# One unrolled stream of 96 attention units, with the feed-forward in pieces between later units, for a cross-attention and six-layer transformer kernel

## What is computed

```python
x = x + xattn(layernorm(x), ctx)              # 16 batch elements, 128 tokens, 128 features
x = x + ffn_stack(layernorm(x))
# ffn_stack:
for i in range(6):
    x = attn_layer(shift_tokens(x), Wqkv[i], q_scale[i], k_scale[i], Wo[i]) + x
    x = ffn_layer(shift_tokens(x), ln_g[i], ln_b[i], W1[i], b1[i], W2[i], b2[i]) + x
# shift_tokens: the upper 64 features of a token are those of the token before it
# attn_layer: 16 heads of 64; q and k l2-normalised, scaled, rotary; each token sees itself and
#   the 32 before it; softmax; times v; times Wo (1024 x 128)
# ffn_layer: layernorm, W1 (128 x 682), a * gelu(gate), W2 (341 x 128)
```

## Time and profile before

| | |
|---|---|
| three runs | median 2150.25 us (2150.19 to 2153.46) |
| profiled execution, first to last instruction (span) | 2147.6 us |
| PE busy | 2027.4 us, 94% |
| DVE busy | 1735.7 us, 81% |
| ACT busy | 1552.4 us, 72% |
| POOL busy | 1353.9 us, 63% |
| DMA | 21.08 MB, mean 10 GB/s |
| mean granted clock of PE | 0.977 of 2.4 GHz |

### The profile page before, as it was taken

How to read it: one execution, slowest core, us unless ns; L and a number is a source line. 1 busy time by engine, 2 the same in 40 slices (tenths; PEclk the granted TensorE clock), 3 DMA queues, 4 the chain that set the end, 5 groups by cost and what they waited for, 6 DMA issues and landing times.

```text
span 2147.6 us, 44268 instructions
## 1 busy us (share of the span) xinstructions
PE 2027.4 (94%) x14352; PEld 1593.7 (74%) x14352; DVE 1735.7 (81%) x3845; ACT 1552.4 (72%) x4966; POOL 1353.9 (63%) x1884
## 2 busy tenths in 40 slices
PE   7699999899999889999999999988999999999997
PEld 5477777777777767777777777776777777777776
DVE  4688887788888678888778888867888867888876
ACT  3488887378888558888738888846888864888873
POOL 2477666466766547777547666745766664766661
PEclk8799999999999999999999999999999999999999
DMA  3000000000000010000010000001000000000000
GB/s 98 30 9 0 0 0 1 17 36 1 0 0 0 11 35 9 0 0 0 1 44 9 0 0 0 0 11 35 9 0 0 0 4 11 1 0 0 0 0 20
DMA packets 11920, 21.08 MB, mean 10 GB/s; under 512 B 1659, under 2 KB 9518, under 8 KB 11054
## 3 DMA queue, kind: packets, MB, share of 16 engines
q1 hardware_dynamic: 11822, 19.77, 2.9%
HBM read 18.72 MB, written 1.05 MB: 9 GB/s over the span
## 4 chain that ended last, share of the span: by engine, by line
PE 68%; DVE 14%; ACT 7%; issue 6%; POOL 4%; DVEq 0%; DMA 0%; ACTq 0%; SPq 0%; POOLq 0%
PE ps L371 15%; PE ps L378 7%; PE ps L351 7%; PE ps L389 7%; PE ps L359 6%; ACT pr L633 6%; PE ps L397 5%; PE ps L353 5%; PE ps L352 5%; PE ps L367 3%; PE ps L520 3%; DVE nmax L966 3%; DVE xs L924 1%; PE ps L341 1%; DVE hT L1052 1%
## 5 line engine op out<-in xcount | busy, mean ns | idle before, releaser
L633 ACT ACTIVATE pr<-ps,nbias,rn 128x128 f32<-128x128 f32 x1536 | 682.4, 454 | 204.6 <-DVE nbias L970 199.4
L784 POOL TENSOR_TENSOR pr<-pr,rsum 128x512 f32<-128x512 f32 x384 | 395.4, 1039 | 304.0 <-DVE rsum L974 304.0
L759 POOL TENSOR_TENSOR t<-t 128x512 f32<-128x512 f32 x384 | 485.1, 1273 | 65.3 <-DVE t L950 59.1
L371 PE MATMUL ps<-kT,qT 64*128 64x128 f32 x3072 | 445.1, 285 | 0.0
L371 PEld LDWEIGHTS ps<-kT,qT 64*128 64x128 f32 x3072 | 371.6, 188 | 97.5 <-issue 97.5
L966 DVE TENSOR_REDUCE nmax<-ps 128x4 f32<-128x512 f32 x384 | 258.7, 674 | 67.2 <-PE ps L371 67.1
L633 ACT ACTIVATION_READ_ACCUMULATOR pr<-ps,nbias,rn 128x1 f32 x1536 | 306.3, 199 | 0.0
L351 PE MATMUL ps<-w_hi,xt_hi 128*128 128x512 f32 x576 | 280.5, 487 | 23.1 <-DVE t L950 18.1
L948 DVE TENSOR_TENSOR t<-ps,rope 128x512 f32<-128x512 f32 x384 | 261.2, 680 | 8.7 <-ACT sq L609 8.7
L950 DVE TENSOR_TENSOR t<-ps,rope 128x512 f32<-128x512 f32 x384 | 260.5, 678 | 0.0
L934 DVE TENSOR_REDUCE ss<-sq 128x8 f32<-128x512 f32 x384 | 248.8, 667 | 3.5 <-issue 2.6
(11 more groups left out here) (116 smaller groups left out, 3173.9 us busy)
## 6 DMA issues: line engine op xcount, KB each, us to landing
wqkv<-wqkv_in SPq DMA_DIRECT2D x6, 1536.0 KB, 8.4
wo<-wo_in SPq DMA_DIRECT2D x6, 512.0 KB, 3.6
w<-w_in SPq DMA_DIRECT2D x6, 342.0 KB, 3.0
w<-w_in SPq DMA_DIRECT2D x6, 172.5 KB
x<-x_in SPq DMA_DIRECT2D x4, 256.0 KB, 4.2
out<-x SPq DMA_DIRECT2D x4, 256.0 KB, 2.3
ctx<-ctx_in SPq DMA_DIRECT2D x4, 240.0 KB, 3.8
qks<-qk_scale_in SPq DMA_DIRECT2D x6, 64.0 KB, 2.8
```

The source lines that it names most:

```text
L371: i = mm(ps[:, o, k * P:(k + 1) * P], qT[r, par, h // 2, :], kT[r, par, h // 2, :], start=False, stop=k == 3, skip_group_check=True)
L633: i = A(pr[:, g, k, :], ps[:, S_BANK[g], k * P:(k + 1) * P], ACT.Exp, bias=nbias[:, g, k:k + 1], scale=rn[:, par, g // 2, 0, 2 * k + g % 2 ...
L759: G.tensor_tensor(t1[:, c, :], t1[:, c, :], t2[:, c, :], ALU.add).then_inc(qk_added[c], 1)
L784: G.tensor_tensor(w, w, rsum[:, g, :].unsqueeze(2).broadcast_to([P, 4, P]), ALU.mult).then_inc(pr_ready[g], 1)
```

## The change

- **One stream.** The layer loops and their special first and last steps go. Steps s = -4 to 107 are unrolled. Step s holds pieces of units s to s-3, of any layer: unit u has layer u // 16. `bank_free` and the waits take unit numbers.
- **Feed-forward between units.** A quad f (0 to 23) has its pieces at fixed distances: its shift and its transposition in step 4f+6, statistics to the first gate in 4f+7, gates 1 and 2 in 4f+8, `ffn_down` in 4f+10, the residual in 4f+11; the next layer's input is transposed for a whole quad in 4f+12. Since the engines' steps are not aligned, DVE's `ffn_stats` (step 4f+7) stands ahead of PE's `ffn_transpose` (step 4f+6).
- **Scores on two row halves.** `scores(u, h2)` makes the two mask products of a half (two banks), and then the eight heads in the order even, odd, even, odd. `row_max` and `inverse_sum` take both banks of a half at once (1024 columns).
- **Token shift by DMA.** SP copies the quad's residual into `xsh`: 64 features of 127 partitions, one partition down, and 64 features of 128 partitions. PE's two shift products and the shifted identity go. DVE's `copy_x` goes too: PE transposes `xr` directly, a quad at a time.
- **Tables.** `ffn_gate` loads Gelu's tables ahead of chunk 0 and the set with Exp and Ln after chunk 2; in between exponentials and norms of attention units are run.
- **Weights.** The next layer's split of Wqkv moves from POOL into the last unit of a layer: high parts on ACT, low parts on DVE (Q0, Q1, V0) and POOL.
- **Copies.** DVE takes six of the 512-column copies of a unit (before four), ACT six (before eight).
- **SP's order.** Weight loads and shift copies share SP's one queue in a fixed order.

```diff
-            def scores(l, b, par, g):
...
-                mm(ps[:, o, :], ident16[:], band16[:].rearrange("p a k -> p (a k)"), start=True, stop=False, skip_group_check=True)
-                for k in range(4):
-                    h = head(g, k)
-                    r = slice(E * (h % 2), E * (h % 2) + E)
...
+            def scores(u, h2):
+
+                pe.wait_ge(tq_ready[2 * h2], u + 1)
+                pe.wait_ge(tq_ready[2 * h2 + 1], u + 1)
+                for odd in range(2):
+                    mm(ps[:, S_BANK[odd], :], ident16[:], band16[:].rearrange("p a k -> p (a k)"), start=True, stop=False,
+                       skip_group_check=True)
+                for k in range(4):
+                    for odd in range(2):
+                        r = slice(E * odd, E * odd + E)
+                        i = mm(ps[:, S_BANK[odd], k * P:(k + 1) * P], qT[r, par(u), 4 * h2 + k, :], kT[r, par(u), 4 * h2 + k, :],
+                               start=False, stop=k == 3, skip_group_check=True)
+                        if k == 3:
+                            i.then_inc(s_ps[h2], 1)
...
+            def shift_tokens(f):
+
+                s = slice(f % NQ * QUAD, f % NQ * QUAD + QUAD)
+                sp.wait_ge(x_updated, f * QUAD + QUAD)
+                if f >= 1:
+                    sp.wait_ge(f_xh, f)
+                else:
+                    sp.wait_ge(const_ready, 9)
+                sp.dma_start(xsh[1:P, :, E:P], xr[0:P - 1, s, E:P]).then_inc(f_shifted, 16)
+                sp.dma_start(xsh[:, :, 0:E], xr[:, s, 0:E]).then_inc(f_shifted, 16)
...
-            with sp.Fori(1, L) as l:
-                wait_apart(sp, w_ready, l * 6)
-                sp.dma_start(wqkv[:], wqkv_d[l]).then_inc(ld_qkv, 16)
...
+            for l in range(L):
+                if l >= 1:
+                    load_rest(l)
+                if l + 1 < L:
+                    load_qkv(l + 1)
+                    load_scales(l + 1)
+                shift_tokens(NQ * l)
+                shift_tokens(NQ * l + 1)
+                if l + 1 < L:
+                    load_w1(l + 1)
+                shift_tokens(NQ * l + 2)
+                if l + 1 < L:
+                    load_wo(l + 1)
+                shift_tokens(NQ * l + 3)
...
+            def load_rest(l):
+                if l >= 1:
+                    sp.wait_ge(f_y_ps, l * NQ)
+                    sp.wait_ge(f_h, l * NQ * FCH)
+                sp.dma_start(w2[:], w2_d[l]).then_inc(ld_ffn, 16)
+                sp.dma_start(vec[:], vec_d[l]).then_inc(ld_ffn, 16)
...
-            def ffn_shift(l, q):
...
-                mm(o[:, :, 0:E], ident, xr[:, s, 0:E], start=True, stop=True)
-                mm(o[:, :, E:P], shift, xr[:, s, E:P], start=True, stop=True).then_inc(f_shift_ps, 1)
...
+            def ffn_gate(f, c):
+                if c == 0:
+                    nc.scalar.preload_act_table(ACT.Gelu)
+                j = f * FCH + c
+                act.wait_ge(f_h_ps, j + 1)
+                A(gate[:, j % 2, :], ps[0:FC, GATE_BANK, :], ACT.Gelu, bias=vec[0:FC, 2 + FCH + c:3 + FCH + c]).then_inc(f_gate, 1)
+                if c == FCH - 1:
+                    nc.scalar.preload_act_table_set("natural_log_exp_and_others")
...
+            def ffn_stats(f):
+                dve.wait_ge(f_shifted, 32 * (f + 1))
+                for b in range(QUAD):
+                    V.bn_stats(st[:, f % 2, b, :], xsh[:, b, :]).then_inc(f_stats, 1)
+                dve.wait_ge(f_stats, 4 * (f + 1))
+                aggregate(f).then_inc(f_var, 1)
...
+            def upper_w(u, c):
+
+                if u % B == B - 1 and u + 1 < UNITS:
+                    l = layer_of(u) + 1
+                    w = slice(CHUNK_COLS[c], CHUNK_COLS[c] + 512)
+                    act.wait_ge(ld_qkv, 16 * (l + 1))
+                    act.wait_ge(qkv_ps[c], u + 1)
+                    A(w_hi[:, w], wqkv[:, w], ACT.Copy).then_inc(w_hi_ready[c], 1)
```

The steps of DVE, as written in the change (the numbers are the distances s - u or s - 4f):

```diff
+            def step(s):
+                run_input(s, 15, lower_xt)
+                run_quad(s, 7, ffn_stats)
+                run(s, 2, row_max, 1)
+                run(s, 1, rotary, K1)
+                run(s, 3, copy_o, 0)
+                run_quad(s, 7, ffn_normalise)
+                run(s, 1, rotary, Q1)
+                run(s, 1, lower_w, Q1)
+                run_quad(s, 7, ffn_affine)
+                run(s, 1, sum_squares, Q1)
+                run(s, 1, sum_squares, K1)
+                run_quad(s, 8, ffn_gated, 1)
+                run(s, 1, copy_qk, K0)
+                run(s, 3, copy_o, 1)
+                run(s, 1, clamp_norm, 1)
+                run(s, 1, copy_v, 0)
+                run(s, 0, rotary, Q0)
+                run(s, 0, lower_w, Q0)
+                run(s, 1, row_max, 0)
+                run_quad(s, 7, ffn_lower)
+                run(s, 2, inverse_sum, 1)
+                run(s, 0, rotary, K0)
+                run(s, 2, copy_pT, 1)
+                run(s, 1, lower_w, V0)
+                run(s, 3, add_residual)
+                run(s, 0, sum_squares, K0)
+                run(s, 1, copy_qk, K1)
+                run(s, 0, sum_squares, Q0)
+                run_quad(s, 11, ffn_residual)
+                run(s, 0, clamp_norm, 0)
+                run(s, 1, inverse_sum, 0)
+                run_quad(s, 7, ffn_gated, 0)
+                run_quad(s, 8, ffn_gated, 2)
+                for l in range(1, L):
+                    if at(s, -8, l):
+                        rope_tables(l)
```

More of the change, by code:

```diff
@@ L199, in bank_free @@
-    def bank_free(eng, l, i, *users):
-        for semaphore, lag in users:
-            if live(i, lag):
-                eng.wait_ge(semaphore, nth(l, i - lag))
-                return
-    def x_ahead(i):
-        return isinstance(i, int) and i <= 1
-    def first_element(b):
-        return isinstance(b, int) and b == 0
-    def last_step(i):
-        return isinstance(i, int) and i == STEPS - 1
-    def steps(eng, l, step):
-        for i in range(1, HEAD_STEPS):
-            step(l, i, i % 2)
-        with eng.Fori(0, (STEPS - HEAD_STEPS - TAIL_STEPS) // 2) as j:
-            step(l, 2 * j + HEAD_STEPS, 0)
-            step(l, 2 * j + (HEAD_STEPS + 1), 1)
-        for i in range(STEPS - TAIL_STEPS, STEPS):
-            step(l, i, i % 2)
@@ L227, in all_layers @@
[L227 to L236 removed]
+    f_shifted, f_stats, f_var, f_sum, f_rstd, f_xh, f_xhT_ps, f_xhT, f_h_ps, f_gate, f_h, f_y_ps = (
+        sem("f_" + s) for s in ("shifted", "stats", "var", "sum", "rstd", "xh", "xhT_ps", "xhT", "h_ps", "gate", "h", "y_ps"))
+    c_stats, c_var, c_sum_eps, c_rstd, c_xn, c_tr_ps, c_tr, c_qk_ps, c_qk, c_s_ps, c_max, c_exp, c_sum, c_pn, c_pT_ps, c_pT, c_o_ps, c_x1 = (
+        sem("c_" + s) for s in ("stats", "var", "sum_eps", "rstd", "xn", "tr_ps", "tr", "qk_ps", "qk", "s_ps", "max", "exp", "sum", "pn",
+                                "pT_ps", "pT", "o_ps", "x1"))
@@ new lines, in build, with live, run, due @@
+    f_hi, f_lo, w1_hi_ready, w1_ready = sem("f_hi"), sem("f_lo"), sem("w1_hi_ready"), sem("w1_ready")
+    final_sum, stored = sem("final_sum"), sem("stored")
+    FIRST_STEP, LAST_STEP = -4, 108
+    def live(s, lag):
+        return 0 <= s - lag < UNITS
+    def run(s, lag, task, *args):
+        if live(s, lag):
+            task(s - lag, *args)
+    def due(s, lag, first=0, last=QUADS):
+        return (s - lag) % QUAD == 0 and first <= (s - lag) // QUAD < last
+    def run_quad(s, lag, task, *args):
+        if due(s, lag):
+            task((s - lag) // QUAD, *args)
@@ new lines, in step @@
+            def step(s):
+                run(s, 0, rotate, K0)
+                run(s, 0, lower_w, K0)
+                run(s, 2, normalise_p, 3)
+                run(s, 0, rotate, Q0)
+                run_quad(s, 6, ffn_power)
+                run(s, 1, normalise_p, 0)
+                run(s, 0, refine_norm, 0)
+                run(s, 1, normalise_p, 1)
+                run(s, 0, normalise_k, 0)
+                run(s, 0, rotate, K1)
+                run(s, 0, lower_w, K1)
+                run(s, 0, rotate, Q1)
+                run(s, 1, lower_w, V1)
+                run(s, 0, refine_norm, 1)
+                run(s, 0, normalise_k, 1)
+                run(s, 1, normalise_p, 2)
+                for l in range(L):
+                    if at(s, 5, l):
+                        split_w1(l)
@@ L838, in _ @@
-            pool.wait_ge(const_ready, 8)
-            step(0, 0, 0)
-            all_layers(pool, layer)
+                    split_first_weights(c)
+                    split_first_weights(c + 1)
+            pool.wait_ge(const_ready, 9)
+            for s in range(FIRST_STEP, LAST_STEP):
+                step(s)
         @block.vector
@@ L1121, in add_input @@
-            def add_input(q):
-                s = slice(q * QUAD, (q + 1) * QUAD)
-                dve.wait_ge(x_final, L * NQ + q + 1)
-                V.tensor_tensor(x1[:, s, :], x1[:, s, :], xr[:, s, :], ALU.add).then_inc(final_sum, 1)
-            rope_tables(0)
-            copy_x(0, 0, 0)
```

(8 more changed lines are left out.)

1033 lines of the change are left out of this document (453 added, 580 removed).

## The result

| | before | after |
|---|---|---|
| median of the runs | 2150.7 us (2150.19 to 2153.46, 4 runs) | 2326.1 us (2316.83 to 2327.28, 4 runs) |
| span of the profiled execution | 2147.6 us | 2322.5 us |
| mean granted clock of PE | 0.977 | 0.910 |

The change makes the kernel **slower by 8.1%**: ratio 1.081, 95% interval 1.079 to 1.084. The forecast was slower by 1.2%, 2176 us, within 1990 to 2290.

The account below looks back on a forecast made before the run. PE was taken as the bound, with DVE and ACT not far below. Start 120, units 1492, feed-forward 188, pauses 253, SP's queue 74, weight split 15 and end 31.6 gave 2174, so 2176 us, range 1990 to 2290.

Parts of the forecast that it names:

- the pause: PE idle 9.0 us a quad awaiting shift copy, statistics and normalisation, plus 2 us of lower clock: 11.0 a quad.
- L: Shift copy from issue to landing: 540 packets, 10.6 us, plus 1.3 fixed, 11.9 us; bounds 6.9 and 16.5.
- SP's queue: Shift copies delayed on SP behind the loads of W2, Wqkv and Wo: together 74 us.
- The sum below, at 82 us a quad, would be the same with either: ACT's eight table loads a quad, at 1.30 or about 2.66 us each, fit within the 82 us quad.
- rival A: Copy spreads over 16 engines and is hidden: 1933 us, or 2020 if ACT with loads sets the pace; chance 0.13.
- I halve the 4% of waits elsewhere to 2%: Waits outside the pause: engines catch up in it, so PE's units and feed-forward are multiplied by 1.02.
- PE's 15.4: PE's work for one attention unit after the change: 15.4 us, with a half's eight score heads at 1.03.
- DVE, too light: DVE's work: 14.5 us an attention unit, 0.7 of it small operations, and 7.9 for a quad's pieces.
- The split of Wqkv and the ends: Weight split in a layer's last unit: 15 us in all; first output projection ends at 120, tail 31.6.
- B: One DMA engine, but small packets inside SBUF at 10.4 ns: copy lands in 6.9 us, 2056 us total; chance 0.20.
- C: Scores' row halves don't overlap: 16 records take 1.81, 1.56 us more a unit, 2326 us total; chance 0.10.
- my line through two rows: Shift copy's packet time, from 62 ns at 1536 bytes and 28 ns at 512: about 20 ns for 256 bytes.

Follow-up runs that it names:

- experiment 4: The changed kernel without table loads in its steps: the gate computes Exp in place of Gelu and both preloads go; 2227.7 us, ratio 1.037.
- experiment 3: The changed kernel with each layer's first shift copy issued ahead of the loads of W2 and Wqkv; 2257.8 us, ratio 1.051.
- Experiment 7: Three runs of the changed kernel: row maximum over every second key, 2259.3 us; no mask products, 2323.0 us; exponentials that don't sum their row, 2256.6 us.
- Experiment 6: The changed kernel with a half's scores ordered four even heads, then four odd, so neighbours no longer alternate row halves; 2365.7 us, ratio 1.099.

## Why the prediction was wrong

The direction and the pause were right; the size was not, since two terms were too small, one of them zero. Term by term, for the span (2174 forecast, 2322.5 found):

- **The pause, right as a sum.** Forecast 11.0 us a quad. Found: 88.4 - 4 x 16.4 (plain) - 8.2 (feed-forward) - 4.0 (loads; this quad takes 84.3 in experiment 4) = 10.6. PE stood still first at `transpose_p`, not ahead of `ffn_transpose`. Its parts were off, and that they cancelled is luck. L is 9.6, not 11.9: a packet of 256 bytes at 18 GB/s takes 14 ns and not 19.7, so the 540 take 7.6 us and 2.0 are left for the rest, for 10.6 and 1.3 in the sum. And from statistics to transposition it took 8.3 us, not 6.0, nearly all of it the normalisation (3.55 for 1.4). With 14 ns and the rest of the working as it stands, the forecast would have been 2103, clearly faster: the direction too owes something to luck. (The sum has one slip: a packet of 16 ns gives 2129, not 2090, which goes with some 13 ns.)
- **SP's queue, right.** 74 forecast; experiment 3 gives 68. The first copies stood 10.4 us behind the residual.
- **"The sum below, at 82 us a quad, would be the same with either": the step that failed first.** I compared ACT's 68 us with the cycle of 82 and costed eight loads at nothing. Each load lies in one of two steps, and in these ACT was busy for 21.2 of 23.2 us and for 17.2 of 18.6. The other two steps' slack is of no use to it. Measured: 98 us for all (experiment 4). The working had this number under rival A (about 21 against PE's 17.3), for the case without a pause, but the pause ends before the loads begin: it cannot cover them. Of the Trainium skill's two figures ("ScalarE: Activation LUTs", section "What ACT_TABLE_LOAD costs") the trace bears out the load's 1.28 us; a drain of 1.38 with each is not seen here, the gate follows its load at once:

```profile
759.71 1.28 ACT L663 ACT_TABLE_LOAD   x1
761.00 0.69 ACT L666 ACTIVATE gate<-ps,vec 114x512 f32<-114x512 f32 x1
```

  With either figure the sum would have needed ACT step by step.
- **"I halve the 4% of waits elsewhere to 2%": the second.** A plain step takes 16.4, 6% over PE's 15.4: 95 x 0.7 = 66 us. Experiment 7 shows that the step is a round trip in which PE, ACT and DVE wait for each other: it gets shorter with less on PE or on ACT, hardly with less on DVE. Before, a group of scores filled one bank while the other was read; now a half takes both. That this exchange makes the round trip longer is read from the order and the chain and is not shown; a version with halves in banks of their own was not tried. Experiment 6 gives what the alternation is worth here: 1.1 us a unit of PE's work and 40 us in all.
- **DVE, too light.** I had 14.5 us a unit; the plain step has 15.6. Its 18 large operations (10.8) and the maxima (3.0) are as forecast, the small ones take 1.8 in place of 0.7, half of it one clamp that lasts 0.99 us beside an operation of POOL. DVE isn't the bound of the plain step; most of the 67 us that 1.2 us less a unit gave came off the step with the pause.
- **The split of Wqkv and the ends.** A layer's third quad takes 3.2 us more than its second and the fourth 1.1, 5 times: 21 against 15. The first output projection ended at 127.4, not 120, and the tail took 38.3, not 31.6.
- **The sum again.** 98 for the loads, 66 for the plain steps, 6 for the split and 14 for the ends are to be added, 6 (SP's queue) and 9 (pauses) taken off, and 19 more since the last quad, with no unit behind it, takes 69.5 us where 88.4 stood. This gives 2324, against 2322.5.

Rivals: A is false. B is false in time: its 10.4 ns a packet were 14, and the rest took 2.0 where it had 1.3, so that L was 9.6 and not 6.9. C is false (halves at 1.09); that its 2326 is the measured time is chance. The Trainium skill's rule behind B ("DMA: Bandwidth & Descriptors", section "Why small descriptors are slow (HBM only)") comes nearer than my line through two rows: a packet took 14 ns, where W2's rate gives 10.4 and the line 19.7. Without the two terms of 98 and 66 us the time would be 2162, hardly above the 2150.7 of before: most of the loss is from terms that no rival had for this case.

## What to carry to other kernels

Compare engines step by step, not by their sums over a cycle: work bunched in one step is covered only by that step. When two groups of results are merged to please one engine, follow who hands the buffers back, and price the round trip. A small DMA between two in-order engines costs what it takes beyond the work queued between issue and use: here 9.6 us cost 6.2 a quad, and 4.65 us nothing. Moving the consumer a step later gave 170 us and widening the copy 141; the two together were not run. The wide copy sends 112 of its 127 partitions, 16 x 7, in one DMA, and the same bytes landed in less than half the time.

## What was not expected of the hardware

- **DVE held up by POOL.** The four normalisations took 3.55 us; from PSUM they took 1.37 before, with POOL at work beside them, and the last quad's, with POOL idle, 1.11. POOL's rows beside them:

```profile
653.27 1.04 POOL L785 TENSOR_TENSOR pr<-pr,rsum 128x512 f32<-128x512 f32 x1
654.27 1.04 POOL L780 TENSOR_TENSOR t<-t,rn 128x512 f32<-128x512 f32 x1
655.26 1.26 POOL L760 TENSOR_TENSOR t<-t 128x512 f32<-128x512 f32 x1
```

  DVE's four run from 653.06 to 656.61; the second, third and fourth each end 0.08 us behind one of these three. The Trainium skill, "SBUF — State Buffer", section "🔬 SBUF: two separate sides", says that GpSimd and VectorE share a pair of ports that an operation holds until it ends, for some kinds of DVE operation; the rows agree. The change had moved the source from PSUM to SBUF. No run took POOL's work away there.
- **A DMA on one engine holds up its queue.** The next DMA's issue took SP 6.4 us behind it (12.8 at most, in a first quad behind W2 and Wqkv as well), 0.9 behind the wide one.
- **The clock.** The granted clock over the step with the pause is 0.83, with no copy at all 0.93, and 1.00 in the other three steps of the quad shown, in which PE is busy for 0.81 to 0.96 of the time.
